# Both silu of a state-space block computed by ScalarE in one step, and a small projection spread over two phases into another PSUM bank

## The chip, the cores and the metric

The kernel runs on one core of a Trainium2 chip. The metric is the device time in microseconds (us), the median of three runs. The core has TensorE (PE), VectorE (DVE), ScalarE (ACT), GpSimd (POOL) and SyncE (SP), which issues the DMAs. Each works through its own list of instructions in order and waits on semaphores.

## The reference

All data is fp32. There are B = 4 batches of L = 512 tokens, model width E = 512, 16 states per channel.

```python
# block 1: selective scan, gated by z
z   = layernorm(x)                                  # per token
u   = silu(causal_conv4(in_proj(ctx)) + conv_b)     # 512 channels
dt, Bm, Cm = split(x_proj @ u)                      # 16 + 16 + 16 rows: the small projection
delta = softplus(dt_proj @ dt + dt_b)
state = state * exp(delta * A) + delta * u * Bm     # for each of 16 states, along 512 tokens
y   = sum_n(state * Cm) + D * u
x   = x + tanh(g_xattn) * (y * silu(z))
# block 2: a gated low-rank mixture of 32, top 2 of a softmax
h   = layernorm(x)
g   = top2(softmax(h @ Wr))
x   = x + tanh(g_ffn) * ((h @ U) * g) @ V * (0.9 + 0.2 * gate)
```

## The kernel before

The work of block 1 is cut into 20 phases f. Phases 0 to 11 take one batch b and one group k of 128 channels over all 512 tokens; the last batch is done in two halves of 256 tokens (phases 12 to 19). A phase has 16 positions n, one for each state. At each position ACT computes the decay (L1007, `exp`), DVE runs the scan (L1262), and the term added comes either from PE (`make_dbu`, L748, into one of three PSUM banks `p_s`) or from POOL (L558, a pair of states at once). POOL multiplies the scanned pair by C (L573; some pairs are done by DVE, L1280), and PE turns and sums it into `p_y` (L770). Which engine does which pair is a fixed table. Rings tie the engines together: three banks `p_s`, three buffers `da` for decays, twelve slots `state`, two buffers `dbu` on POOL.

Everything else is written by hand into a position of these phases: for the phase after it the dt projection (PE, n = 4), softplus (ACT, n = 6 to 8) and `delta` (DVE, L1221, n = 7); for the block five phases on the in-projection (PE, n = 9), the start of the convolution (ACT, L924, n = 12) and its three taps (DVE, L1204, n = 10 to 12); and block 2 of tile f - 5 or f - 6 (scores, top 2, products with U and V).

The two silu are made by halves, as v * (1 + tanh(v)) on halved inputs, since tanh lies in the same activation table as `exp`. For z, ACT writes `zh` (L1026) at n = 13 and `tanh` into the bank `p_v` (L1031) at n = 14, and DVE multiplies them at n = 14 (L1285). For u, ACT writes `tanh` into the bank `p_pr` (L933) and DVE multiplies (L1212), both at n = 15. The first four blocks of u are exceptions: they use the Silu function before the phases begin.

Phases 3, 7 and 11 are the last of their batch ("turning"). In them PE computes the small projection of the next batch (four products, L680, two at n = 1 and two at n = 2) into `p_pr`, ACT copies it to `xd` at n = 5 (L941), PE's dt projection waits for that copy at n = 4 (L692), and POOL writes diagonals of B (L531) and the scale of z (`scale_of_z`, L579 to L589, six small operations).

## Time and profile before

| | |
|---|---|
| median of 3 runs | 539.43 us (539.42 to 541.25) |
| the profiled execution | 541.24 us, its span 539.4 us |
| PE busy | 489.4 us, 91% of the span |
| DVE busy | 476.8 us, 88% |
| POOL busy | 454.4 us, 84% |
| ACT busy | 398.6 us, 74% |

The engines share the span almost evenly: no engine is idle for long between the first phase and the last, and a busy share says little without the stretch it comes from. The DMA queues move 73 GB/s on average and are quiet in most stretches. The busy time of PE counts its matmuls; weight loads run beside them.

### The profile page before, as it was taken

How to read it: one execution, taken by the hardware profiler on the slowest of the kernel's cores; microseconds unless marked ns; L12 is line 12 of the kernel's file. 1: busy time of each engine (PE TensorE's matmuls, PEld its weight loads, DVE VectorE, ACT ScalarE, POOL GpSimd, SP SyncE). 2: the span in 40 equal slices, each digit the busy share in tenths (PEclk: the TensorE clock that was granted, in tenths of full speed). 3: DMA queues.
4: the chain of work that ended last, by engine and by line, in shares of the span. 5: the costliest groups of instructions: out<-in, count | busy, mean ns of one | idle time of the engine just before them, and what ended most of it. 6: DMA issues, size and time to landing. Idle time of an engine off the chain costs nothing.

```text
span 539.4 us, 9244 instructions
## 1 busy us (share of the span) xinstructions
PE 489.4 (91%) x3018; PEld 367.8 (68%) x3018; DVE 476.8 (88%) x880; ACT 398.6 (74%) x726; POOL 454.4 (84%) x335
## 2 busy tenths in 40 slices
PE   9989798979677999999989999999899999899687
PEld 5569597758475776668677776667566666676654
DVE  3799999879899999789999999888988989999851
ACT  4698869386867777587968777577888898888542
POOL 1299999959999999979999999989799898987810
PEclk9979999999998999999998999999999999999799
DMA  5595001055220001074120000087000000000001
GB/s 134 161 373 215 0 2 40 2 200 192 82 78 2 1 0 60 7 280 169 59 80 2 19 2 21 5 299 227 22 21 1 21 20 21 2 20 21 1 19 39
DMA packets 18705, 39.36 MB, mean 73 GB/s; under 512 B 5586, under 2 KB 6354, under 8 KB 18659
## 3 DMA queue, kind: packets, MB, share of 16 engines
q1 hardware_dynamic: 18658, 38.79, 21.1%
q8 instruction: 24, 0.39, 0.3%
q14 instruction: 23, 0.18, 0.1%
HBM read 34.33 MB, written 4.46 MB: 72 GB/s over the span
## 4 chain that ended last, share of the span: by engine, by line
PE 54%; DVE 19%; ACT 18%; issue 8%; DVEq 0%; POOL 0%; ACTq 0%; POOLq 0%
PE p_s L748 12%; PE p_y L770 11%; DVE state L1262 9%; PE p_v L803 8%; PE p_f L794 6%; ACT da L1007 4%; PE p_tr L717 4%; PE p_pr L692 2%; PE p_pr L680 2%; DVE p_s L1262 2%; ACT p_s L1007 2%; DVE x L1204 2%; ACT pair_b L991 2%; PE p_pr L673 2%; PE p_f L783 2%
## 5 line engine op out<-in xcount | busy, mean ns | idle before, releaser
L573 POOL TENSOR_TENSOR state<-state,c_bc 128x1024 f32<-128x1024 f32 (+1 forms) x131 | 256.7, 1973 | 21.5 <-DVE state L1262 19.2
L748 PEld LDWEIGHTS p_s<-pair_b,du_t 128*128 128x128 f32 x1072 | 139.2, 198 | 44.7 <-issue 31.4
L748 PE MATMUL p_s<-pair_b,du_t 128*128 128x128 f32 x1072 | 153.1, 285 | 16.7 <-DVE state L1262 13.8
L770 PE MATMUL p_y<-ident,state 128*128 128x128 f32 x1024 | 149.5, 276 | 0.0
L558 POOL TENSOR_TENSOR dbu<-du,pair_b 128x1024 f32<-128x1024 f32 (+1 forms) x80 | 145.3, 1818 | 1.7 <-DVE p_s L1262 1.7
L1007 ACT ACTIVATE p_s<-delta,a_neg 128x512 f32<-128x512 f32 (+1 forms) x162 | 93.5, 580 | 65.8 <-DVE state L1280 33.0
L1262 DVE TENSOR_TENSOR_SCAN state<-da,p_s 128x512 f32<-128x512 f32 (+1 forms) x116 | 134.4, 1173 | 6.3 <-PE p_s L748 5.7
L770 PEld LDWEIGHTS p_y<-ident,state 128*128 128x128 f32 x1024 | 121.6, 144 | 23.7 <-issue 22.7
L1007 ACT ACTIVATE da<-delta,a_neg 128x512 f32<-128x512 f32 (+1 forms) x158 | 100.4, 648 | 14.0 <-DVE state L1262 13.7
L1262 DVE TENSOR_TENSOR_SCAN state<-p_s,dbu 128x512 f32<-128x512 f32 (+1 forms) x100 | 98.2, 997 | 1.8 <-POOL dbu L558 1.8
L794 PE MATMUL p_f<-u_sb,h_t 128*128 128x512 f32 x112 | 55.9, 602 | 0.5 <-DVE gw L1365 0.5
L803 PE MATMUL p_v<-v_sb,hug_t 128*128 128x512 f32 x112 | 55.3, 597 | 0.0
L1280 DVE TENSOR_TENSOR state<-p_s,c_bc 128x256 f32<-128x256 f32 (+1 forms) x58 | 30.6, 527 | 0.7
L531 POOL TENSOR_SCALAR_AFFINE_SELECT pair_b<-b_t 128x1024 f32<-128x1024 f32 x11 | 12.4, 1132 | 20.5 <-ACT b_t L964 20.5
L1262 DVE TENSOR_TENSOR_SCAN state<-p_s,carry,dbu 128x256 f32<-128x256 f32 x40 | 28.0, 735 | 0.5 <-POOL dbu L558 0.4
L1262 DVE TENSOR_TENSOR_SCAN p_s<-p_s,dbu 128x512 f32<-128x512 f32 x22 | 26.8, 1218 | 0.0
L794 PEld LDWEIGHTS p_f<-u_sb,h_t 128*128 128x128 f32 x112 | 18.8, 194 | 10.8 <-issue 9.8
L964 ACT ACTIVATE sz_t<-p_tr 128x512 f32<-128x512 f32 (+1 forms) x20 | 10.1, 507 | 21.4 <-PE p_tr L717 21.2
L1204 DVE SCALAR_TENSOR_TENSOR vsp<-p_pr,cw,vsp 128x511 f32<-128x511 f32 (+2 forms) x33 | 24.1, 731 | 1.1 <-ACT vsp L924 1.1
L759 PEld LDWEIGHTS p_y<-ident,skipped 128*128 128x128 f32 x64 | 7.3, 142 | 25.5 <-issue 25.5
L673 PE MATMUL p_pr<-cx,w_in 128*128 128x512 f32 x44 | 21.1, 601 | 3.4 <-DVE delta L1221 3.4
L1007 ACT ACT_TABLE_LOAD x18 | 23.1, 1283 | 0.3
(182 smaller groups left out, 687.8 us busy)
## 6 DMA issues: line engine op xcount, KB each, us to landing
c_bc<-bc_rows SPq DMA_DIRECT2D x32, 512.0 KB, 5.2
pair_b<-bc_rows SPq DMA_DIRECT2D x16, 512.0 KB, 5.7
xs<-in_x SPq DMA_DIRECT2D x16, 256.0 KB, 4.0
out<-ot SPq DMA_DIRECT2D x14, 256.0 KB, 2.0
cx<-in_ctx_t SPq DMA_DIRECT2D x4, 512.0 KB, 3.5
u_sb<-in_u_w SPq DMA_DIRECT2D x1, 1024.0 KB, 14.2
v_sb<-in_v_w SPq DMA_DIRECT2D x1, 1024.0 KB, 15.6
w_in<-in_in_w_t SPq DMA_DIRECT2D x1, 384.0 KB, 4.6
```

The lines of the kernel that those rows point to most:

```text
L558: eng.tensor_tensor(dbu[:, i % 2, :, 0:w], du[:, 0:w].unsqueeze(1).to_broadcast([P, 2, w]), rows_of_b(p)[:, :, c0:c0 + w], ALU.mult).then_ ...
L573: eng.tensor_tensor(pair, pair, c_bc[:, 2 * p:2 * p + 2, c0:c0 + w], ALU.mult).then_inc(po_cs, 1)
L673: mm = eng.matmul(conv_bank(q)[:, :], w_in[:, k, e * P:(e + 1) * P], cx[:, k, :], start=(k == 0), stop=(k == KD - 1))
L717: mm = eng.transpose(turn_bank(kind, i)[:, k, :], source[:, k * P:(k + 1) * P], ident[:, :])
L748: mm = eng.matmul(p_s[g % BANKS][:, t * P:(t + 1) * P], du_t[:, f % 2, t, :], diagonals_of(n // 2)[:, n % 2, c0 // P + t, :], start=(t == ...
L770: mm = eng.matmul(p_y[:, t, :], slot(NS * f + n)[:, t * P:(t + 1) * P], ident[:, :], is_transpose=True, start=False, stop=(n == NS - 1 and ...
L794: mm = eng.matmul(hu_bank(T)[:, :], ht_of(T)[:, k, :], u_sb[:, k, :], start=(k == 0), stop=(k == Q - 1))
L803: mm = eng.matmul(v_bank(T)[:, :], hugt_of(T)[:, k, :], v_sb[:, k, :], start=False, stop=(k == Q - 1), skip_group_check=True)
L1007: eng.activation(to, delta[:, f % 2, 0:w], ACT.Exp, scale=a_neg[:, k, n:n + 1]).then_inc(ac_da, 1)
L1204: eng.scalar_tensor_tensor(out=conv_v(q)[:, s:], in0=conv_bank(q)[:, 0:L - s], scalar=cw[:, q % Q, TAPS - 1 - s:TAPS - s], in1=conv_v(q)[: ...
L1262: eng.tensor_tensor_scan(scanned, decayed, added, first, ALU.mult, ALU.add).then_inc(ve_scan, 1)
L1280: eng.tensor_tensor(slot(g)[:, 0:w], scanned, c_bc[:, n, c0:c0 + w], ALU.mult).then_inc(ve_cs, 1)
```

## The change

Both silu are now one ScalarE instruction with the function Silu, which needs a table of its own. `silu(f)` loads the Silu table, does one or two blocks of z and up to two of u, and loads a table back that holds `exp` and `ln` together. It stands in 15 of the 20 phases: at n = 0 in phase 1 and in the turning phases, at n = 9 in the others, and only in every second phase of the last batch, with two blocks of z. DVE's two multiplications are gone, and ACT's `zh`, `tanh` of z and `tanh` of u with them. The convolution is now done in the slot of `u` itself, in a ring of 5 instead of 6. `tanh(g_xattn)` is no longer folded into the scale of z (`scale_of_z` has four operations instead of six) but applied where `sz_t` is copied.

The small projection of the next batch goes into `p_v`: three of its products stand at n = 13, 14 and 15 of the phase before the turning one, the fourth at n = 2 of the turning phase. `copy_small` moves from n = 5 to n = 4, the dt projection of a turning phase from n = 4 to n = 5, and `place_residual`, which starts the product with V in `p_v`, follows `copy_small`. Two small operations on `cw` and `cb` ahead of the phases are gone.

```diff
+    SILU_Z = {1: [0, 1]}
+    SILU_Z.update({f: [f] for f in range(2, SPLIT)})
+    SILU_Z.update({f: [f, f + 1] for f in range(SPLIT, F, 2)})
+    SILU_U = {1: [5], 2: [4, 6]}
+    SILU_U.update({f: [f + 4] for f in range(3, SPLIT)})
...
-            return x2[:, q // Q, q % Q, :] if q < 5 else vsp[:, :]
+            return x2[:, q // Q, q % Q, :] if q < 5 else u[:, q % U_RING, :]
...
             def scale_of_z(b):
...
-                eng.tensor_tensor(zv[:, 1, :], zv[:, 0, :], minus_half[:, :], ALU.pow).then_inc(po_zs, 1)
+                eng.tensor_tensor(zr[:, b % 2, 0, :], zv[:, 0, :], minus_half[:, :], ALU.pow).then_inc(po_zs, 1)
                 eng.wait_ge(po_zs, ZOPS * b + 2)
-                eng.tensor_tensor(zr[:, b % 2, 0, :], zv[:, 1, :], half[:, :], ALU.mult).then_inc(po_zs, 1)
-                eng.tensor_tensor(zv[:, 0, :], zv[:, 1, :], minus_half[:, :], ALU.mult).then_inc(po_zs, 1)
-                eng.wait_ge(po_zs, ZOPS * b + 4)
-                eng.tensor_tensor(zr[:, b % 2, 1, :], zmv[:, :, 0], zv[:, 0, :], ALU.mult).then_inc(po_zs, 1)
-                eng.wait_ge(po_zs, ZOPS * b + 5)
-                eng.wait_ge(ac_k, 2)
-                eng.tensor_scalar(zr[:, b % 2, 2:4, :], zr[:, b % 2, 0:2, :], gx[:, :], None, ALU.mult).then_inc(po_zs, 1)
+                eng.tensor_tensor(zv[:, 1, :], zmv[:, :, 0], zr[:, b % 2, 0, :], ALU.mult).then_inc(po_zs, 1)
+                eng.wait_ge(po_zs, ZOPS * b + 3)
+                eng.tensor_tensor(zr[:, b % 2, 1, :], zv[:, 1, :], minus_one[:, :], ALU.mult).then_inc(po_zs, 1)
...
@@ PE, small_projection and the phases
-                    wait_for_u(eng, Q * b + Q if b else k + 1)
-                    mm = eng.matmul(p_pr[0:BROW + 2 * NS, :], w_small[:, k, :], u[:, (Q * b + k) % U_RING, :],
+                    eng.wait_ge(ac_u, Q * b + k + 1)
+                    if b and k == 0 and Q * b - 8 >= 0:
+                        eng.wait_ge(ac_out, Q * b - 7)
+                    mm = eng.matmul(small_bank(b)[0:BROW + 2 * NS, :], w_small[:, k, :], u[:, (Q * b + k) % U_RING, :],
...
-                        if turning:
-                            small_projection(b + 1, range(0, 2))
...
-                            small_projection(b + 1, range(2, Q))
+                            small_projection(b + 1, [Q - 1])
...
-                    if n == 4 and f < LAST:
+                    if n == (5 if turning else 4) and f < LAST:
                         dt_projection(f + 1)
+                    if n >= 13 and k == Q - 2 and b + 1 < B:
+                        small_projection(b + 1, [n - 13])
...
@@ ACT
+            def silu_z(f):
...
+                eng.activation(zh_of(f), xs[:, b % 2, k, c0:c0 + w], ACT.Silu, bias=zr[:, b % 2, 1, k:k + 1],
+                               scale=zr[:, b % 2, 0, k:k + 1]).then_inc(ac_z, 1)
+            def silu(f):
+                eng.preload_act_table(ACT.Silu)
+                for i in SILU_Z[f]:
+                    silu_z(i)
+                for q in SILU_U.get(f, []):
+                    silu_u(q)
+                eng.preload_act_table_set("natural_log_exp_and_others")
...
+                    if n == 4 and turning:
+                        copy_small(b + 1)
+                        if tail >= 0:
+                            place_residual(tail)
...
-                    if n == 13:
-                        z_part(f, 0)
-                    if n == 14:
-                        z_part(f, 1)
...
-                        if f + 5 < BLOCKS:
-                            tanh_v(f + 5)
+                    if f in SILU_Z and n == (0 if f == 1 or turning else 9):
+                        silu(f)
...
@@ DVE
-                        silu_z(f)
...
-                    if f == 0 and n == 15:
-                        silu_u(4)
-                    if n == 15 and f + 5 < BLOCKS:
-                        silu_u(f + 5)
```

How the instructions then stand. First ACT in phase 6, from the second part of softplus for phase 7 to the start of the next convolution; `vsp` is softplus, `da` and `p_s` are decays, `skipped` is D * u. Before:

```order
201 L955 ACTIVATE vsp<-vsp 128x512
202 L1007 ACTIVATE da<-delta,a_neg 128x512
203 L958 ACT_TABLE_LOAD
204 L958 ACTIVATE vsp<-vsp 128x512
205 L1007 ACT_TABLE_LOAD
206 L1007 ACTIVATE da<-delta,a_neg 128x512
207 L1015 ACTIVATE skipped<-u,dsk 128x512
208 L1007 ACTIVATE p_s<-delta,a_neg 128x512
209 L1086 ACTIVATE ot<-p_v 128x512
```

The same place of the changed kernel:

```order
186 L963 ACTIVATE vsp<-vsp 128x512
187 L1016 ACTIVATE da<-delta,a_neg 128x512
188 L966 ACTIVATE vsp<-vsp 128x512
189 L1016 ACTIVATE da<-delta,a_neg 128x512
190 L1024 ACTIVATE skipped<-u,dsk 128x512
191 L1038 ACT_TABLE_LOAD
192 L1033 ACTIVATE zh<-xs,zr 128x512
193 L941 ACTIVATE u<-u 128x512
194 L1043 ACT_TABLE_LOAD
195 L1016 ACTIVATE p_s<-delta,a_neg 128x512
196 L1102 ACTIVATE ot<-p_v 128x512
```

The two table loads moved from around the last part of softplus to behind `skipped`, with the two silu between them, ahead of the decay of position 10.

Second, PE from the end of phase 6 into phase 7, a turning phase; `p_s<-pair_b,du_t` is `make_dbu`, `p_y<-ident,state` the sum of y, `p_tr` the transposes, `w_small` the small projection. Before:

```order
202 L717 MATMUL p_tr<-ident,du 128x128 x4
203 L770 MATMUL p_y<-ident,state 128x128 x8
204 L717 MATMUL p_tr<-ident,h 128x128 x4
205 L748 MATMUL p_s<-pair_b,du_t 128x128 x4
206 L770 MATMUL p_y<-ident,state 128x128 x4
207 L748 MATMUL p_s<-pair_b,du_t 128x128 x4
208 L770 MATMUL p_y<-ident,state 128x128 x4
209 L680 MATMUL p_pr<-u,w_small 64x512 x2
210 L770 MATMUL p_y<-ident,state 128x128 x4
211 L680 MATMUL p_pr<-u,w_small 64x512 x2
212 L717 MATMUL p_tr<-ident,zh 128x128 x4
213 L783 MATMUL p_f<-router,h_t 128x32 x4
```

The same place of the changed kernel:

```order
203 L691 MATMUL p_v<-u,w_small 64x512
204 L728 MATMUL p_tr<-ident,du 128x128 x4
205 L781 MATMUL p_y<-ident,state 128x128 x4
206 L691 MATMUL p_v<-u,w_small 64x512
207 L781 MATMUL p_y<-ident,state 128x128 x4
208 L691 MATMUL p_v<-u,w_small 64x512
209 L728 MATMUL p_tr<-ident,h 128x128 x4
210 L759 MATMUL p_s<-pair_b,du_t 128x128 x4
211 L781 MATMUL p_y<-ident,state 128x128 x4
212 L759 MATMUL p_s<-pair_b,du_t 128x128 x4
213 L781 MATMUL p_y<-ident,state 128x128 x8
214 L691 MATMUL p_v<-u,w_small 64x512
```

Three products of the small projection moved ahead of the first `make_dbu` of the turning phase; the fourth stays ahead of the scores.

## Rows read from the trace of the kernel before

**Rows 1.** The windows view, cut where DVE starts `delta` (L1221, position 7 of a phase).
```profile
core 0: us, PE busy (x) PEld busy (x) DVE busy (x) ACT busy (x) POOL busy (x), PEclk, DMA share, GB/s
63.26:87.24 23.98, 22.05 (x178) 19.69 (x177) 23.79 (x27) 19.05 (x29) 23.98 (x12) 1.00 0.01 2
87.24:117.25 30.01, 27.62 (x197) 21.79 (x195) 25.61 (x29) 20.32 (x31) 24.49 (x12) 1.00 0.19 66
...
173.96:202.58 28.62, 27.53 (x180) 21.42 (x179) 28.30 (x48) 21.35 (x35) 28.01 (x15) 1.00 0.00 1
202.58:234.15 31.57, 29.98 (x181) 20.99 (x181) 28.42 (x49) 22.87 (x38) 27.68 (x14) 1.00 0.20 74
...
324.06:355.18 31.12, 29.54 (x181) 20.97 (x180) 28.41 (x48) 22.40 (x39) 27.69 (x14) 1.00 0.15 49
...
380.69:488.94 108.25, 101.95 (x582) 70.55 (x581) 99.22 (x272) 93.45 (x199) 94.50 (x107) 1.00 0.04 16
```

**Rows 2.** The waits of POOL: releaser, us in total, times, longest.
```profile
POOL state L573 <- DVE state L1262: 19.2, 18, 5.5
POOL fr L596 <- DVE fmv L1317: 11.0, 3, 5.7
```

**Rows 3.** POOL's timeline: start, duration, and in brackets the idle time before.
```profile
113.33 2.36 POOL L573 TENSOR_TENSOR state<-state,c_bc 128x1024 f32<-128x1024 f32 x1 [5.52 <-DVE state L1262]
...
230.72 2.35 POOL L573 TENSOR_TENSOR state<-state,c_bc 128x1024 f32<-128x1024 f32 x1 [1.52 <-DVE state L1262]
...
```

**Rows 4.** POOL's timeline over the scale of z in phase 3.
```profile
128.61 0.20 POOL L583 TENSOR_TENSOR zr<-zv,half 128x4 f32<-128x4 f32 x1
...
129.34 0.31 POOL L589 TENSOR_SCALAR zr<-zr,gx 128x8 f32<-128x8 f32 x1
129.61 1.10 POOL L531 TENSOR_SCALAR_AFFINE_SELECT pair_b<-b_t 128x1024 f32<-128x1024 f32 x1
```

**Rows 5.** Groups by line on DVE, PE and ACT: count, busy us, mean ns, idle before.
```profile
L1285 DVE SCALAR_TENSOR_TENSOR zh<-p_v,zh 128x512 f32<-128x512 f32 (+1 forms) x20 | 11.2, 559 | 0.0
L1212 DVE SCALAR_TENSOR_TENSOR u<-p_pr,vsp 128x512 f32<-128x512 f32 x11 | 7.4, 670 | 0.0
L680 PE MATMUL p_pr<-u,w_small 128*64 128x512 f32 x32 | 15.9, 608 | 0.2 <-ACT u L929 0.2
L1007 ACT ACT_TABLE_LOAD x18 | 23.1, 1283 | 0.3
```

**Rows 6.** PE's timeline in phases 6 and 7, with the idle time before each piece.
```profile
215.41 0.65 PE L717 MATMUL p_tr<-ident,h 128*128 128x128 f32 x4 [1.09 <-ACT h L1046]
...
218.66 1.93 PE L680 MATMUL p_pr<-u,w_small 128*64 128x512 f32 x4
...
227.17 1.12 PE L692 MATMUL p_pr<-xd,w_dt 17*128 17x512 f32 x2 [0.49 <-ACT xd L941]
```

**Rows 7.** ACT's timeline in phase 6.
```profile
199.75 1.28 ACT L958 ACT_TABLE_LOAD   x1
201.04 0.63 ACT L958 ACTIVATE vsp<-vsp 128x512 f32<-128x512 f32 x1
...
204.22 0.67 ACT L1007 ACTIVATE p_s<-delta,a_neg 128x512 f32<-128x512 f32 x1
...
206.54 0.76 ACT L924 ACTIVATE vsp<-p_pr,cb,cw 128x512 f32<-128x512 f32 x1
...
207.81 0.81 ACT L1026 ACTIVATE zh<-xs,zr 128x512 f32<-128x512 f32 x1
```

**Rows 8.** DVE's timeline beside it: position 10 and the first tap.
```profile
206.58 1.21 DVE L1262 TENSOR_TENSOR_SCAN state<-p_s,dbu 128x512 f32<-128x512 f32 x1
...
208.29 0.73 DVE L1204 SCALAR_TENSOR_TENSOR vsp<-p_pr,cw,vsp 128x511 f32<-128x511 f32 x1
```

**Rows 9.** The same in phase 2: ACT's start of the convolution, DVE's first tap.
```profile
91.60 0.76 ACT L924 ACTIVATE vsp<-p_pr,cb,cw 128x512 f32<-128x512 f32 x1
92.39 0.75 DVE L1204 SCALAR_TENSOR_TENSOR vsp<-p_pr,cw,vsp 128x511 f32<-128x511 f32 x1
```

133 lines of the change are left out of this document (56 added, 77 removed).

## The prediction

> **What bounds the kernel now.** I read the busy shares first, and they decide nothing: four engines lie between 74% and 91%. So I cut the span into stretches of one phase and compared, in each, its length with every engine's busy time [rows 1]; the reader is to look for the engine whose busy time comes nearest to the length. In phases 1 to 2 (the first stretch) it is POOL, 23.98 of 23.98 us, with DVE at 23.79. In phases 5 to 6 all three are within a hair: DVE 28.30, POOL 28.01 and PE 27.53 of 28.62. In the stretches that enter a turning phase the picture differs: 30.01, 31.57 and 31.12 us long, POOL works only 24.49, 27.68 and 27.69 of them, while PE works 27.62, 29.98 and 29.54. In the last batch (seven half phases, 108.25 us) PE has 101.95, DVE 99.22, POOL 94.50. So no engine is the bound alone: POOL and DVE share it in ordinary phases, PE has it in turning ones and in the last batch.
>
> Next I read the waits of POOL, because POOL is never ahead for long: between the first phase and the last it waits 19.2 us for scans, and 11.0 us for the statistics of block 2, of which 5.7 lie behind the last phase [rows 2]. That is 24.5 us, and the change can gain little more than that, since it takes almost no work from POOL. Its largest single waits are in the turning phases: 5.52 us in phase 3, and in phase 7 the longest of several is 1.52 [rows 3].
>
> **The change part by part.**
>
> *DVE loses the two multiplications.* 20 of z, 11.2 us, and 12 of u (11 in the row, one more of the same size), 8.1 us [rows 5]: 19.3 us of busy time. A full phase loses 2 x 0.67, and since neighbours on DVE overlap by some 0.08 each, 1.17 us; a half phase about 0.3. In phases 5 to 6 that puts DVE at 27.1 of 28.62, but POOL's 28.01 stays: the phase can shorten by 0.6, not by 1.17. In phases 1 to 2 it can shorten by nothing. Over the six ordinary full phases 4 to 6 and 8 to 10 the bounds are 0 and 6 x 1.17 = 7.0; I take **-2.0**, nearer to POOL's row than to DVE's.
>
> *POOL loses two of six operations of the scale of z.* From L583 to the diagonal behind L589 are 129.61 - 128.61 = 1.00 us for four operations [rows 4]; two small ones, the second waiting for the first, take some 0.55. That is 0.45 in each of three turning phases, on the engine that has no idle time just behind them: **-1.35**. The fourth scale stands ahead of the phases beside other work and counts nothing.
>
> *The small projection.* Two of its products take 1.93 us on PE, less 0.07 of overlap [rows 6], so all four take 3.7 (the mean of one part is 608 ns before overlap, two parts to a product [rows 5]), and 2.8 of that moves to n = 13 to 15 of the phase before. This removes no PE work, and PE has no lead to hide it in: it feeds a ring of three banks. The stretch that enters phase 7 holds both the old and the new place and PE's 29.98 us fill it to 1.59. What the move can give is that idle time: PE waited 1.09 us for `h` just ahead of phase 7's first `make_dbu`, and 0.49 for `xd` ahead of the dt projection [rows 6]. With two products ahead of the transpose of `h`, and `tanh` of u gone from ACT ahead of `h`, the first wait is covered; with `xd` copied one position earlier and the dt projection one later, so is the second. I count 1.6 for phase 7 and the same for phase 11 (31.12 - 29.54). In phase 3 the stretch leaves PE 2.4 us, but part of what ended POOL's wait of 5.52 there is the scans of positions 3 to 5, and ACT will be late (below), so I count 0.7, with bounds of 0 and 2.4. Together **-3.9**. If the first wait were not covered, each of the later two would give 0.5 less than 1.
>
> *ACT.* Before, 37 table loads in the phases (18 ahead of `exp` [rows 5], as many ahead of `ln`, one in phase 0), now 30; each holds ACT 1.29 us (199.75 to 201.04) [rows 7]. The two loads stay in an ordinary full phase, but move from around the last part of softplus to behind `skipped`, and bring silu of z (like L1026, 0.70 after overlap) and of u (like L958, 0.53). So the decay of position 10 comes 1.3 us later than now relative to position 6. In phase 6 it is ready at 204.89 and its scan begins at 206.58, a cover of 1.7 [rows 7, 8]: enough. The convolution's start ends at 207.30, the tap that needs it begins at 208.29, a cover of 1.0: DVE is late by 0.3. In phase 2 two blocks of u are in the group, 1.85 us more, and the cover is 0.03 (92.36 to 92.39) [rows 9]: DVE loses about 1.9 there, against 1.17 gained. In the turning phases the group of 3.9 us stands behind the decay of position 0; what is queued behind it is the decay of position 1, for which DVE waits, and behind that the copies of `h` and `sz`. PE comes late at the same place by its 2.8 us, so the two lie side by side. In the last batch half of the loads go and ACT gains. POOL's full queue in phases 1 to 2 absorbs part of phase 2's loss. Bounds 0 and 1.9 + 6 x 0.3 = 3.7, I take **+1.0**.
>
> The Trainium skill states another price for the loads: in "ScalarE: Activation LUTs", What ACT_TABLE_LOAD costs, about 1283 ns and then about 1380 ns of drain for each switch. The trace agrees with the first (1.28) and shows no second: the instruction behind the load begins at its end. By that rule a group would hold ACT 2.8 us longer than I count.
>
> *The last batch.* PE idles 108.25 - 101.95 = 6.3 us in it; part of that is waiting for scans or for ACT's copies. DVE loses 0.3 and ACT about 1.8 us a half phase (one load of 1.28, and two writes of `zh` and `tanh` made one). Bounds 0 and 6.3, I take a third: **-2.1**.
>
> *At nothing:* the ring of u at 5 (its last reader stands three positions ahead of the write, on the same engine, and POOL's read is a phase old), the scale in the copy of `sz_t` (another [128,1] operand, some 0.1 us on ACT, eight positions ahead of its use), `place_residual` behind `copy_small`, and the two small DVE operations ahead of the phases, where ACT decides.
>
> **Sum:** -2.0 - 1.35 - 3.9 + 1.0 - 2.1 = -8.35 us. The profiled execution took 541.24, 1.8 above the median of the runs; it would come to 532.9, and the median to **531**.
>
> **The rivals.**
>
> *DVE's whole cut arrives.* For it: in phases 5 to 6 DVE is busier than POOL. Against it: POOL's 23.98 of 23.98 in phases 1 to 2. It gives about 11 x 1.17 + 8 x 0.3 = 15 us, the scale 1.35, and the waits of PE at the turns 3: 520.
>
> *Almost nothing arrives.* PE's work is the same to the last matmul, and it fills 94 to 95% of the turning stretches and of the last batch. If its remaining 1.6 and 6.3 us are the price of handing over between engines and not waits that go away, only -1.35 and half of the ordinary phases' 2.0 remain, and ACT's +1.0 against them: 538.
>
> *ACT's group becomes the new stall (slower).* Place: n = 10 of the ordinary full phases and n = 1 of the turning ones. For it: the covers of 0.03 and 1.0. Against it: in phase 6 the group costs only 0.3 beyond its cover. Price: if each of the eleven groups of phases 1 to 11 made DVE wait as in phase 2, 1.9 each, the loss is 21, the DVE cut there 11 x 1.17 = 12.9, the turns and the scale 5.3: +3, 542.5 or more. It decides from the point where a group delays the tap by more than the cover of 1.0 and DVE's 1.17 together, that is when it holds ACT 2.2 us longer than the loads do now, not 1.3. The drain of the page cited above would do just that.
>
> **How the numbers follow.** The sum as described 0.68 (its own range 527 to 535.5), the whole DVE cut 0.06, almost nothing 0.17, slower 0.09. 0.5% is 2.7 us, about what a measurement of this kernel can tell from no change: faster means under 536.7, slower over 542.1. A few hundredths of the third case fall below 536.7 and of the fourth below 542.1: faster 0.76, same 0.16, slower 0.08. The range leaves out the second case, half of the fourth and some of both edges: 526 to 539.
>
> **What the profile after would show.** DVE busy down by 17 to 19 us; 30 table loads in the phases, each followed at once by its activation. The stretches entering phases 7 and 11 at 30 us or a little under, with no wait of PE for `h` or `xd`; the one entering phase 3 shorter by 1 to 2. Phases 1 to 2 not shorter, with DVE waiting 1 to 2 us for ACT's convolution in phase 2. Ordinary full phases 0 to 0.6 us shorter with POOL as good as never idle. The last batch at 106. Wrong would be: POOL idle in ordinary phases (then ACT or PE, not POOL, took over from DVE), DVE waiting for decays at n = 10 or 11 in most phases, or a turning stretch that stays at 31.

## The result and the profile after

The changed kernel takes **534.03 us** (median of 4 runs, 533.25 to 534.77), the kernel before beside it 539.59 (4 runs): ratio 0.9881, 95% interval 0.9856 to 0.9906. That is 5.6 us less by the medians, 6.4 by the ratio, and 0.9 to 1.4% by the interval. The forecast was 531, with a range of 526 to 539. The profiled execution took 533.53, 7.7 less than that of before; the sum had said 8.35 less.

The page of the kernel after, its busy times:

```profile
span 531.8 us, 9178 instructions
PE 491.4 (92%) x3018; PEld 368.0 (69%) x3018; DVE 462.9 (87%) x846; ACT 380.1 (71%) x699; POOL 451.9 (85%) x327
```

DVE's busy time fell by 13.9 us (476.8 to 462.9), ACT's by 18.5, PE's and POOL's hardly. The windows view of the kernel after, cut as in [rows 1] where DVE starts `delta`, now L1226. The first two stretches run from there in the start to position 7 of phase 0 and of phase 1; the last is what lies behind the last cut.

```profile
core 0: us, PE busy (x) PEld busy (x) DVE busy (x) ACT busy (x) POOL busy (x), PEclk, DMA share, GB/s
23.17:39.16 15.99, 13.68 (x66) 11.31 (x65) 15.22 (x18) 13.83 (x33) 13.69 (x11) 0.68 1.01 356
39.16:66.06 26.90, 24.62 (x172) 21.99 (x171) 22.35 (x25) 21.82 (x38) 25.68 (x12) 0.88 0.32 118
90.03:119.06 29.03, 27.57 (x194) 21.26 (x193) 24.57 (x27) 22.77 (x34) 22.30 (x12) 1.00 0.16 50
174.64:203.36 28.72, 27.66 (x180) 21.19 (x179) 27.07 (x46) 22.08 (x35) 28.45 (x16) 1.00 0.00 1
203.36:234.04 30.68, 30.68 (x183) 20.98 (x182) 27.22 (x46) 23.30 (x37) 29.22 (x15) 1.00 0.24 84
320.12:351.49 31.37, 31.37 (x189) 21.85 (x188) 27.33 (x47) 24.15 (x39) 28.15 (x15) 1.00 0.21 66
375.20:482.93 107.73, 101.74 (x582) 70.62 (x581) 97.73 (x268) 84.17 (x187) 95.02 (x107) 1.00 0.04 16
482.93:531.80 48.87, 39.96 (x204) 27.39 (x202) 29.88 (x79) 22.77 (x50) 20.94 (x20) 0.97 0.06 22
```

Two stretches of the kernel before that [rows 1] doesn't hold, in the same view: the first two.

```profile
23.78:38.26 14.48, 11.80 (x68) 10.29 (x67) 13.83 (x17) 13.61 (x32) 14.15 (x12) 0.76 1.02 345
38.26:63.26 25.00, 23.22 (x182) 20.32 (x181) 23.87 (x29) 21.00 (x38) 24.38 (x12) 1.00 0.40 151
```

Two stretches got longer by more than 0.3 us, and the forecast had looked at neither: the one of phase 0 by 1.5 us and the one of phases 0 to 1 by 1.9. In the turning stretches of phases 7 and 11 PE fills the stretch to the last hundredth (30.68 of 30.68, 31.37 of 31.37). The table cuts the whole profiled span of five kernels in this way; three are experiments below ("DVE cut alone" is the kernel before without the two multiplications, so that silu is left out and tanh alone stands in its place, "DVE work back" the kernel after with DVE's load of before, "both repairs" the kernel after mended at two places). A turning stretch stands together with the one behind it, for the runs showed that a gain in one is often taken back in the other.

| stretch (phases) | before | DVE cut alone | after | DVE work back | both repairs |
|---|---|---|---|---|---|
| start, to `delta` of phase 0 | 23.78 | 23.14 | 23.17 | 23.81 | 23.20 |
| 0 | 14.48 | 15.59 | 15.99 | 15.99 | 14.96 |
| 0 to 1 | 25.00 | 23.20 | 26.90 | 26.34 | 23.23 |
| 1 to 2 | 23.98 | 23.98 | 23.97 | 23.80 | 23.58 |
| 2 to 4 (turn at 3) | 57.22 | 56.07 | 56.09 | 56.12 | 56.09 |
| 4 to 6 | 58.12 | 57.88 | 57.24 | 61.01 | 57.25 |
| 6 to 8 (turn at 7) | 62.02 | 61.54 | 59.41 | 60.61 | 59.95 |
| 8 to 10 | 59.46 | 57.53 | 57.35 | 59.70 | 57.34 |
| 10 to 12 (turn at 11) | 56.63 | 56.46 | 55.08 | 54.66 | 55.23 |
| last batch | 108.25 | 107.95 | 107.73 | 108.85 | 107.61 |
| behind it | 50.46 | 49.36 | 48.87 | 49.21 | 49.26 |
| span | 539.4 | 532.7 | 531.8 | 540.1 | 527.7 |

POOL's waits after, against [rows 2]:

```profile
POOL state L586 <- DVE state L1267: 19.2, 19, 4.8
POOL fr L605 <- DVE fmv L1316: 9.2, 3, 4.4
```

POOL waits as long for scans as before. So the time did not come out of these waits, on which the argument for a small gain had rested. What POOL has less is 2.5 us of busy time, 1.8 of waits for the statistics of block 2, and 1.7 us of waits for DVE ahead of its own products, which are gone.

**Where phase 1 lost.** ACT's and DVE's timelines of the kernel after, in phase 1:

```profile
50.39 1.28 ACT L1038 ACT_TABLE_LOAD   x1
51.69 1.52 ACT L1033 ACTIVATE zh<-xs,zr 128x512 f32<-128x512 f32 x2
53.12 0.61 ACT L941 ACTIVATE u<-u 128x512 f32<-128x512 f32 x1
53.75 1.28 ACT L1043 ACT_TABLE_LOAD   x1
55.04 1.95 ACT L1016 ACTIVATE da<-delta,a_neg 128x512 f32<-128x512 f32 x3
...
55.85 1.22 DVE L1267 TENSOR_TENSOR_SCAN state<-da,p_s 128x512 f32<-128x512 f32 x1 [2.12 <-PE p_s L759]
```

The view names PE's `p_s` as releaser, but the scan starts 0.16 us behind the end of the first of ACT's three decays at 55.04, and that decay stands behind the group of 4.6 us (two loads, silu of z twice, silu of u). DVE waits 2.12 us at this place. The timeline also shows what a load costs: 1.28 us, and the activation starts at its end.

PE waits in its turn, 2.17 us for the scan, and then works at a clock that differs from one kernel to the next. Its first `make_dbu` behind this wait, in the kernel after and in the one with POOL's wait (below):

```profile
60.28 2.05 PE L759 MATMUL p_s<-pair_b,du_t 128*128 128x128 f32 x8 [2.17 <-DVE state L1267]
...
59.85 1.13 PE L760 MATMUL p_s<-pair_b,du_t 128*128 128x128 f32 x8 [2.17 <-DVE state L1268]
```

In the first the granted clock is 0.50 from 60 to 66 us, the lower level of 1.2 GHz, and DVE waits another 1.34 and 0.28 us for `p_s`; in the second it stays at 1.00 and DVE waits no more. The stretch of phases 0 to 1 takes 26.90 us in the first and 25.34 in the second, with the same group at the same place. So of the 3.7 us that the kernel after loses here against DVE's cut alone (23.20), about 2.1 are the wait behind the group and about 1.6 the lower clock behind it.

### The profile page after: what moved, and what is told of

The parts are those of the page before. It is cut to its first block, busy times and chain, and to the rows that moved or that the text cites. A ratio compares the mean times of both kernels' runs of the same rounds, so it can differ in the third digit from the quotient of the medians.

```text
span 531.8 us, 9178 instructions
## 1 busy us (share of the span) xinstructions
PE 491.4 (92%) x3018; PEld 368.0 (69%) x3018; DVE 462.9 (87%) x846; ACT 380.1 (71%) x699; POOL 451.9 (85%) x327
## 4 chain that ended last, share of the span: by engine, by line
PE 48%; POOL 19%; DVE 13%; ACT 10%; issue 9%; DMA 1%; DVEq 0%; SPq 0%; POOLq 0%; ACTq 0%
PE p_s L759 12%; PE p_y L781 11%; POOL state L586 9%; POOL dbu L571 7%; DVE state L1267 6%; PE p_v L814 5%; PE p_f L805 5%; PE p_tr L728 3%; PE p_v L691 2%; ACT da L1016 2%; DVE x L1216 2%; PE p_pr L703 2%; ACT pair_b L1000 1%; PE p_f L794 1%; PE p_pr L682 1%
## 5 line engine op out<-in xcount | busy, mean ns | idle before, releaser
L759 PEld LDWEIGHTS p_s<-pair_b,du_t 128*128 128x128 f32 x1072 | 140.7, 200 | 44.9 <-issue 33.4
L1016 ACT ACTIVATE da<-delta,a_neg 128x512 f32<-128x512 f32 (+1 forms) x158 | 99.3, 647 | 18.5 <-DVE state L1267 18.4
L805 PEld LDWEIGHTS p_f<-u_sb,h_t 128*128 128x128 f32 x112 | 18.5, 191 | 12.7 <-issue 9.6
L1216 DVE SCALAR_TENSOR_TENSOR u<-p_pr,cw,u 128x511 f32<-128x511 f32 (+2 forms) x33 | 24.1, 730 | 2.2 <-ACT u L936 2.1
L814 PEld LDWEIGHTS p_v<-v_sb,hug_t 128*128 128x128 f32 x112 | 18.1, 190 | 8.4 <-issue 8.3
L556 POOL TENSOR_TENSOR du<-delta,u 128x512 f32<-128x512 f32 (+1 forms) x19 | 19.8, 1043 | 2.8 <-POOL dbu L571 2.8
```

The costliest lines, as they stand in the source:

```text
L556: eng.tensor_tensor(du[:, 0:w], delta[:, f % 2, 0:w], u[:, (Q * b + k) % U_RING, c0:c0 + w], ALU.mult).then_inc(po_du, 1)
L759: mm = eng.matmul(p_s[g % BANKS][:, t * P:(t + 1) * P], du_t[:, f % 2, t, :], diagonals_of(n // 2)[:, n % 2, c0 // P + t, :], start=(t == ...
L805: mm = eng.matmul(hu_bank(T)[:, :], ht_of(T)[:, k, :], u_sb[:, k, :], start=(k == 0), stop=(k == Q - 1))
L814: mm = eng.matmul(v_bank(T)[:, :], hugt_of(T)[:, k, :], v_sb[:, k, :], start=False, stop=(k == Q - 1), skip_group_check=True)
L1016: eng.activation(to, delta[:, f % 2, 0:w], ACT.Exp, scale=a_neg[:, k, n:n + 1]).then_inc(ac_da, 1)
L1216: eng.scalar_tensor_tensor(out=conv_v(q)[:, s:], in0=conv_bank(q)[:, 0:L - s], scalar=cw[:, q % Q, TAPS - 1 - s:TAPS - s], in1=conv_v(q)[: ...
```

## The experiments

All ratios are against the kernel before on the same chip (541.5 to 542.2 us there). The kernel after ran again beside three of them (534.27 us, ratio 0.9863: the split group, POOL's wait, and DVE's work with one input in PSUM). It did not run beside "both repairs", "scale of z back" and "DVE's cut alone"; these are compared with 534.27 us and 0.9863 across chips, and medians and ratios then differ by about 1 us.

### Small projection back in the turning phase

```
@@ PE, n loop
+                    if n == 1 and turning:
+                        small_projection(b + 1, range(0, 2))
...
-                            small_projection(b + 1, [Q - 1])
+                            small_projection(b + 1, range(2, Q))
...
-                    if n >= 13 and k == Q - 2 and b + 1 < B:
-                        small_projection(b + 1, [n - 13])
```

> The changed kernel with the small projection back in the turning phases alone, two products at n = 1 and two at n = 2, still in p_v. Theory (the move pays only through PE's waits for h and for xd, some 1.1 and 0.5 us a turn before, since PE's work is the same): +1 to +2 us against the changed kernel, 535 to 536, and PE waits again for h or xd at the turns. Rival (the move is what the change lives on): +4 us or more, 538 or above. Rival (it does nothing, the silu alone do it): within 0.5 us.

Measured 534.56 us, ratio 0.9861 (0.9831 to 0.9891): the same as the kernel after, so the second rival (within 0.5 us) has it. PE does wait again for `h`, 0.57 us in phase 7 and 0.57 in phase 11, as the theory said. In its profile phases 6 to 8 take 60.28 us instead of 59.41, phases 2 to 4 56.19 instead of 56.09, 10 to 12 55.22 instead of 55.08: 1.1 us in all. But 0.9 of it lies in phases 6 to 8, where kernels with the small projection in its new place take anything from 59.41 to 60.09 us. So the profile shows 0.2 us for the spreading of the small products outside that scatter, and the median 0.3 to 0.5.

### DVE's work back, both inputs in SBUF

```
+            def multiply_again(f, w):
+                eng.scalar_tensor_tensor(out=vsp[:, 0:w], in0=delta[:, f % 2, 0:w], scalar=1.0,
+                                         in1=delta[:, f % 2, 0:w], op0=ALU.add, op1=ALU.mult).then_inc(ve_again, 1)
...
+                        multiply_again(f, PHASE[f][3])
...
+                    if n == 15 and f + 5 < BLOCKS:
+                        multiply_again(f, L)
```

> The changed kernel, and DVE does again as much work as before: a multiplication of the same size into a spare buffer at n = 14 of each phase and at n = 15 where u was multiplied (33 in all, 19 us; their result is not used). Theory (DVE was the limit only in part of the ordinary phases, POOL and PE take over): +3 to +5 us, 537 to 539, not 19. Rival (DVE's cut gives nothing, the gain is of the turns and of ACT): below +1. Rival (DVE decides everywhere): +10 or more.

Measured 566.15 us, ratio 1.0450 (1.0397 to 1.0503). By the number that is the last rival's "+10 or more", but three times it, and more than the 19 us of work that was meant to be put back: 32 operations cost 32 us, a full microsecond each. The groups of DVE in its profile show why this was no measure of DVE's cut:

```profile
L1295 DVE SCALAR_TENSOR_TENSOR vsp<-delta 128x512 f32<-128x512 f32 x24 | 35.8, 1493 | 0.2 <-issue 0.2
```

The operation that the change removed took 670 ns at this size [rows 5]; it read one input from PSUM. This one reads both from SBUF and takes 1493 ns in the mean, up to 2830, and POOL's busy time rises with it, from 452.3 us in the experiment before to 463.5, with no work added to POOL. I repeated it with one input in PSUM (further below).

### No table loads in the phases

```
-                eng.activation(u[:, q % U_RING, :], conv_v(q), ACT.Silu).then_inc(ac_u, 1)
+                eng.activation(u[:, q % U_RING, :], conv_v(q), ACT.Silu if q < Q else ACT.Identity).then_inc(ac_u, 1)
...
-                eng.preload_act_table(ACT.Silu)
...
-                eng.preload_act_table_set("natural_log_exp_and_others")
```

> The changed kernel without the 30 table loads of the phases: in them Identity stands in the place of Silu, so silu is left out of the result, and ACT's group at n = 0 or 9 is 2.6 us shorter. Theory (the group makes DVE wait at n = 1 of phase 1 and of the turning phases and at n = 10 of phases 2 and 8, 2.1, 2.0, 1.3, 1.0, 1.0 and 0.7 us in the trace): -4 to -6 us against the changed kernel, 528 to 530. Rival (POOL's queue and PE's work cover these waits): within 1 us.

Measured 531.15 us, ratio 0.9797 (0.9766 to 0.9827). This kernel leaves out silu. It takes 3.4 us less than the first experiment, which ran beside it and equals the kernel after: all 30 loads (38.5 us of ACT) together cost 3.4 us, less than the theory's 4 to 6 and more than the rival's 1. The windows view says where:

```profile
39.64:62.75 23.11, 22.27 (x176) 19.89 (x177) 22.03 (x25) 18.92 (x36) 22.88 (x11) 1.00 0.38 139
199.79:230.49 30.70, 30.70 (x182) 21.00 (x181) 27.45 (x46) 19.59 (x34) 29.12 (x15) 1.00 0.23 82
371.55:479.37 107.82, 101.80 (x582) 70.61 (x581) 97.77 (x267) 76.21 (x182) 94.67 (x107) 1.00 0.04 16
```

Phases 0 to 1 fall from 26.90 to 23.11 us. Phases 6 to 7 stay at 30.70 and the last batch at 107.82, although ACT works 3.7 and 8.0 us less in them. Nearly all that the loads cost is at this one place (3.0 us against the first experiment, whose stretch took 26.15); of the other places where the theory saw DVE wait, phases 8 to 10 come next with 0.5.

### The loads doubled

```
                 eng.preload_act_table(ACT.Silu)
+                eng.preload_act_table_set("natural_log_exp_and_others")
+                eng.preload_act_table(ACT.Silu)
```

> The changed kernel with four table loads in each of the 15 groups instead of two: ACT held 2.6 us longer at each place. Theory (the covers at n = 10 and n = 1 are used up: 0.1 to 0.8 us in the full phases, 0.7 to 1.2 in the last batch): +12 to +25 us, slower than the kernel before. Rival (ACT has 28% of the span idle and the groups are covered elsewhere by POOL and PE): below +6.

Measured 568.49 us, ratio 1.0487 (1.0443 to 1.0531): 34 us for 30 more loads of 1.28, 38.5 us of ACT, beyond the theory's 12 to 25. The groups of ACT, one of the two added lines:

```profile
L1039 ACT ACT_TABLE_LOAD x15 | 19.2, 1283 | 0.1
```

Together with the experiment before, this measures the covers. The first 30 loads cost 3.4 us; the next 30 find the covers used up and cost nearly their own length. The turning stretches, which hold two groups each and so 5.1 us of added loads, grow from 29.03 to 35.00 and from 30.68 to 35.39 us, the ordinary ones of phases 4 to 5 and 5 to 6, with one group, by 3.1 and 1.4. The granted clock in these four is 0.95, 0.90, 0.93 and 0.91, so part of the 34 us is PE at its lower clock; how much was not separated.

### The kernel after once more

> The changed kernel once more, beside the three that follow, so that they are compared on one chip. Every theory: 534 us, give or take 1, and in the profile the same stretches as before: 26.9 us for phase 0 to 1's stretch with DVE idle 4.5 us, 16.0 us for the stretch ahead of it.

Measured 534.27 us (6 runs, 533.44 to 535.12), ratio 0.9863 (0.9839 to 0.9886). Its stretches are those of the table within 0.1 us but for four: the start at 23.64, phases 0 to 1 at 26.39, 1 to 2 at 23.59, and 49.88 behind the last batch. So the two ends of the span differ by 0.5 and 1.0 us between two profiles of one kernel.

### Phase 1's group split and moved

```
-    SILU_Z = {1: [0, 1]}
+    SILU_Z = {0: [0], 1: [1]}
...
-                    if f in SILU_Z and n == (0 if f == 1 or turning else 9):
+                    if f in SILU_Z and n == (0 if turning else 9 if f else 13):
```

> Silu of z of phase 0 goes into a group of its own at n = 13 of phase 0, and phase 1 has its group (z of phase 1, u of block 5) at n = 9 as the other ordinary phases; no group stands at n = 0 of phase 1. One group more, so two table loads more. Theory that the place of phase 1's group costs about 3 us (the scan of n = 1 waited 2.1 us for the decay queued behind it): 531.0 to 532.5, the stretch that holds phase 1 at 23.5 to 24.5 us instead of 26.9, at most 0.7 us given back in phase 0 and at n = 10 of phase 1. Rival, that the ACT work costs the same wherever it stands (the loads in ACT's queue, not their place): 534 to 536.

Measured 532.77 us, ratio 0.9832 (0.9806 to 0.9857): 1.5 us less than the kernel after, just outside the theory's range of 531.0 to 532.5. The stretch of phases 0 to 1 falls by 3.2 us as the theory said, and part of it is given back at two places:

```profile
39.12:62.34 23.22, 21.65 (x173) 19.52 (x174) 22.14 (x25) 20.38 (x36) 22.99 (x11) 1.00 0.36 135
62.34:86.58 24.24, 22.60 (x181) 20.03 (x180) 22.55 (x25) 18.54 (x28) 24.24 (x12) 1.00 0.01 2
171.22:201.18 29.96, 29.39 (x179) 22.52 (x178) 27.33 (x47) 20.58 (x33) 29.69 (x16) 0.92 0.00 1
```

Phases 1 to 2 take 24.24 us instead of 23.59 and DVE idles 1.7 of them: the group at n = 9 of phase 1 is longer than the cover behind it. Phases 5 to 6 take 29.96 instead of 28.72 with the granted clock at 0.92 instead of 1.00, and phases 6 to 7 take 31.36 instead of 30.67.

### POOL's diagonals behind DVE's first products

```
             scale_of_z(0)
+            eng.wait_ge(ve_dbu, 2)
             diagonals(0, 2)
```

> POOL makes its second and third diagonal tile only after DVE's two first products of du and B (one wait of POOL on DVE added; no work changed). In the changed kernel POOL's two fewer operations of the z scale let these diagonals start 1.7 us earlier, beside DVE's two products, which took 1184 and 1570 ns instead of 687. Theory that the two engines take turns at SBUF there, and that this cost the stretch of phase 0 its 1.5 us: the two products at 0.69 each again, the stretch at 14.5 to 15.0 instead of 16.0, 532.5 to 533.5 in all. Rival, that POOL's later start costs as much as DVE gains: 534, same within 0.5.

Measured 533.10 us, ratio 0.9842 (0.9815 to 0.9870). First the timelines of DVE and POOL of the kernel after at this place, and of the kernel before:

```profile
25.32 2.68 DVE L1272 TENSOR_TENSOR dbu<-du,pair_b 128x512 f32<-128x512 f32 x2 [0.73 <-DMA pair_b<-bc_rows]
24.87 2.58 POOL L544 TENSOR_SCALAR_AFFINE_SELECT pair_b<-b_t 128x1024 f32<-128x1024 f32 x2
...
25.81 1.30 DVE L1267 TENSOR_TENSOR dbu<-du,pair_b 128x512 f32<-128x512 f32 x2 [0.61 <-DMA pair_b<-bc_rows]
26.57 2.55 POOL L531 TENSOR_SCALAR_AFFINE_SELECT pair_b<-b_t 128x1024 f32<-128x1024 f32 x2
```

Before, POOL's six operations of the scale of z held its diagonals until 26.57, when DVE's two products were nearly done. After, with four operations, POOL starts them at 24.87, 0.45 ahead of DVE, and DVE's products, with both inputs in SBUF, take 2.68 us instead of 1.30. With the wait they take 1.29 again (DVE, timeline of this experiment), and POOL's two diagonals 2.14:

```profile
26.28 1.29 DVE L1273 TENSOR_TENSOR dbu<-du,pair_b 128x512 f32<-128x512 f32 x2 [1.00 <-DMA pair_b<-bc_rows]
27.65 2.14 POOL L544 TENSOR_SCALAR_AFFINE_SELECT pair_b<-b_t 128x1024 f32<-128x1024 f32 x2 [2.02 <-DVE dbu L1273]
```

The stretch of phase 0 falls from 15.98 to 14.86 us, and the next from 26.39 to 25.34, where PE kept its higher clock (above). The median moved by 1.2 only: in the profiled execution phases 6 to 7 take 31.35 us instead of 30.67, and phases 5 to 6 take 30.10 us instead of 28.72, again with a clock of 0.92. The windows view there, first of this kernel, then of the kernel after once more, 1.9 us later in its span:

```profile
170.00:172.00 2.00, 0.65 (x1) 0.50 (x2) 1.93 (x5) 1.98 (x3) 2.00 (x2) 0.65 0.00 0
172.00:174.00 2.00, 2.00 (x3) 0.66 (x2) 2.00 (x3) 1.97 (x4) 2.00 (x2) 0.50 0.01 4
...
172.00:174.00 2.00, 0.78 (x2) 0.49 (x3) 1.93 (x5) 1.98 (x3) 2.00 (x2) 1.00 0.00 0
174.00:176.00 2.00, 2.00 (x12) 1.34 (x11) 2.00 (x4) 1.97 (x4) 2.00 (x2) 1.00 0.01 4
```

In the one TensorE is granted 0.50, its level of 1.2 GHz, and in the other 1.00, 2.4 GHz. PE had idled 1.71 and 1.47 us just ahead in the one, 1.72 and 1.43 in the other. In the first full 2 us the one has 3 matmuls and the other 12 in the stretch that answers to it.

### DVE's work back, one input in PSUM

```
+            def multiply_again(w):
+                eng.scalar_tensor_tensor(out=vsp[:, 0:w], in0=p_pr[:, 0:w], scalar=1.0,
+                                         in1=vsp[:, 0:w], op0=ALU.add, op1=ALU.mult).then_inc(ve_again, 1)
...
+                    if n == 14 and f < LAST:
+                        multiply_again(PHASE[f + 1][3])
+                    if n == 15 and f + 5 < BLOCKS:
+                        multiply_again(L)
```

> DVE's whole cut put back: 19 multiplications at n = 14 and 11 at n = 15 of the same form as those removed (one input in PSUM, one in SBUF, out to SBUF), on data that nothing else needs; ACT, PE and POOL have the work of the changed kernel. If DVE's cut gave what I forecast for the ordinary phases, and a little elsewhere: 536 to 538, that is 2 to 4 us more. If DVE is the real bound of the ordinary phases: 30 x 0.6 = 17 us more, 545 to 551. If the cut was worth nothing because POOL and PE decide: 534, same within 0.5. DVE busy up by about 17 us in each case.

Measured 542.04 us (12 runs), ratio 1.0021 (1.0001 to 1.0042): **all of the gain is gone**. The time lies between the expectations, above the 536 to 538 of my forecast and below the 545 of DVE as the bound. The group of the added operation on DVE, and the windows of phases 4 to 5 and 6 to 7:

```profile
L1247 DVE SCALAR_TENSOR_TENSOR vsp<-p_pr,vsp 128x512 f32<-128x512 f32 (+1 forms) x30 | 17.8, 594 | 0.0
...
146.06:176.40 30.34, 22.89 (x153) 17.96 (x152) 29.45 (x53) 20.66 (x32) 29.98 (x18) 0.91 0.12 36
207.07:237.75 30.68, 30.68 (x183) 20.98 (x182) 28.51 (x49) 24.77 (x39) 27.69 (x14) 1.00 0.24 85
```

17.8 us of DVE's time cost 7.8 us of the kernel's. In the table, the cost lies in phases 4 to 6 (3.8, of which by my estimate about 1.4 belong to the stretch of phases 5 to 6, with a clock of 0.93 and 30.67 us; that is what the lower clock cost there in the kernel with POOL's wait), 8 to 10 (2.4), 7 to 8 (1.2) and the last batch (1.1). Phases 0 to 1 and 2 to 4 take as long as without it, within 0.1 us. Where phase 7 is entered it costs nothing: 30.68 us with the work and 30.68 without, for PE fills both.

### Both repairs together

The two edits above, with phase 1's group at n = 12 instead of 9:

```
+                    if f in SILU_Z and n == (0 if turning else 9 if f > 1 else 13 - f):
```

> Both repairs together: silu of z of phase 0 in a group at n = 13 of phase 0, phase 1's group at n = 12 (behind the start of the convolution, not ahead of it), and POOL's wait for DVE's first two products. Theory that the two losses are apart from each other: 14.9 us for the stretch of phase 0 (16.0 in the changed kernel) and 23.2 for the next (26.4), with no wait of DVE at n = 10 of phase 1, so 529.5 to 531; up to 2 us of it can go again if TensorE's clock falls to its lower level in phase 5, as it did with either repair alone. Rival, that whatever is gained early is given back at the next turning phase: 532.5 to 534.

Measured **529.21 us** (528.45 to 529.55), ratio 0.9785 (0.9759 to 0.9812). This beats both kernels, 2.15% under the kernel before and 4 to 5 us under the kernel after (4.2 by the ratios, 5.1 by the medians). The windows of its stretches of phase 0 and of phases 1 to 2; the one between them takes 23.23 us:

```profile
23.20:38.16 14.96, 11.57 (x71) 9.68 (x69) 13.82 (x17) 13.82 (x33) 12.60 (x10) 0.89 1.02 353
61.39:84.97 23.58, 22.09 (x178) 19.72 (x178) 23.02 (x25) 18.71 (x28) 23.58 (x11) 1.00 0.01 2
```

POOL works 23.58 of 23.58 us in phases 1 to 2. Phases 5 to 6 stay at 28.73 here, with a clock of 0.96 in them and not 0.92.

### POOL's two operations of the scale of z back

```
                 eng.tensor_tensor(zr[:, b % 2, 1, :], zv[:, 1, :], minus_one[:, :], ALU.mult).then_inc(po_zs, 1)
+                if b:
...
+                    eng.tensor_tensor(z_again[:, 0, :], zr[:, b % 2, 0, :], minus_half[:, :], ALU.mult).then_inc(po_again, 1)
+                    eng.wait_ge(po_again, 2 * b - 1)
...
+                    eng.tensor_scalar(z_again[:, :, :], zr[:, b % 2, :, :], gx[:, :], None, ALU.mult).then_inc(po_again, 1)
```

> The changed kernel with POOL's two fewer operations of the z scale put back for batches 1 to 3, on data that nothing needs (one small product and the product with gx, waits as before the change). My term of -1.35 (0.45 in each of three turning phases): 535.5 to 536, and the stretches from phase 3 to 4, 7 to 8 and 11 to 12 each about 0.45 us (up to 1.0) longer. Rival, that POOL has room there because PE's 30.7 us set the turning phases: 534, same within 0.5.

Measured 535.35 us (534.86 to 535.62), ratio 0.9903 (0.9876 to 0.9929): 1.1 us more than the kernel after by the medians, 2.2 by the ratios, across chips. Phases 3 to 4 grow from 27.05 to 27.63 us and 11 to 12 from 23.74 to 24.30, 7 to 8 not at all (28.75 to 28.77). In the first two POOL hardly idles:

```profile
118.61:146.24 27.63, 22.37 (x170) 19.09 (x169) 24.32 (x27) 19.29 (x35) 27.30 (x21) 1.00 0.57 200
352.30:376.60 24.30, 22.44 (x148) 17.25 (x148) 20.57 (x43) 16.98 (x39) 23.48 (x22) 1.00 0.65 217
```

### The kernel before with DVE's cut alone

```
-                eng.activation(conv_bank(q)[:, :], conv_v(q), ACT.Tanh).then_inc(ac_th, 1)
+                eng.activation(u[:, q % U_RING, :], conv_v(q), ACT.Tanh).then_inc(ac_th, 1)
...
-                        silu_z(f)
...
-                        silu_u(f + 5)
```

> The kernel before with DVE's part of the change alone: its two multiplications are gone and tanh is used in their place, so silu is left out from block 4 of u on and in every gate; all of ACT's loads, the small projection and the z scale stay where they were. Theory that DVE's cut alone is the gain and that the rest of the change nets to nothing: 533 to 535.5, the stretches of phases 4 to 6 and 8 to 10 shorter by 0.6 to 1.2 each, turning stretches by 0.5 at most. Rival, that POOL holds the ordinary phases as I forecast (2.0 us in six): 539 to 540.

Measured 534.72 us, ratio 0.9894 (0.9866 to 0.9922). This kernel leaves out silu: `tanh` alone stands for it in every gate and from block 4 of u on. DVE's cut alone gives 6.9 us by the medians and 5.7 by the ratio, where the whole change gave 7.2 and 7.4 beside the kernel before on another chip. The total is the theory's, the places are only half of them: phases 8 to 10 give 1.9 us, but 4 to 6 only 0.2. Its windows of phases 0 to 1, 3 to 4 and 5 to 6:

```profile
38.73:61.93 23.20, 21.84 (x175) 19.69 (x176) 22.11 (x26) 21.04 (x38) 22.97 (x11) 1.00 0.39 143
115.91:141.98 26.07, 21.26 (x163) 18.39 (x162) 24.31 (x26) 20.74 (x37) 25.74 (x20) 1.00 0.59 205
170.58:199.86 29.28, 28.19 (x179) 21.57 (x178) 27.32 (x46) 21.11 (x35) 29.01 (x16) 0.96 0.00 1
```

### The dt projection back at n = 4

```
-                    if n == (5 if turning else 4) and f < LAST:
+                    if n == 4 and f < LAST:
...
-                    if n == 4 and turning:
-                        copy_small(b + 1)
...
                     if n == 5:
...
+                        if turning:
+                            copy_small(b + 1)
```

> The changed kernel with the dt projection of the turning phases back at n = 4 on PE and the copy of the small projection back at n = 5 on ACT, behind the copy of the gated rows; the residual goes behind it, since it uses the same bank. The turning stretches got 1.0 to 2.6 us shorter by the change, and neither the place of the small products nor the loads nor DVE's cut gave it in the stretch of phases 2 to 3 (29.1, 29.0 there without each of them, 30.0 with DVE's cut alone). Theory that this one position is what took PE's wait for xd away: 535.5 to 537, the stretches entering phases 3, 7 and 11 each 0.5 to 1.0 us longer, and PE waiting about 0.5 us for xd again. Rival, that the wait only shows elsewhere: 534.3, same within 0.5.

Measured 534.39 us, ratio 0.9861 (0.9839 to 0.9883): the same as the kernel after. PE's timeline in phase 3 shows the wait back, as the theory said:

```profile
113.87 1.12 PE L703 MATMUL p_pr<-xd,w_dt 17*128 17x512 f32 x2 [0.89 <-ACT xd L949]
```

The stretch of phases 2 to 3 grows from 29.03 to 29.79 us. But the next falls from 27.06 to 26.30, and phases 2 to 4 take 56.09 with it and without it. The wait was real and removing it gave nothing; the rival was right.

## Why the prediction was right and where it was wrong

The direction and the range were right, and the total missed by 3 us. In the profiled executions, for which the sum was made, it came within 0.6 us (532.9 forecast, 533.53 measured); the other 2.3 us come from taking over that the profiled execution lies 1.8 above the median, as it did before. After, it lies 0.5 below. That the sum came so near is in good part luck, for terms that missed by 0.9 to 1.6 us cancel. They are, in the profiled executions:

| term of the sum | forecast | measured | what the runs say of it |
|---|---|---|---|
| ordinary full phases 4 to 6, 8 to 10 | -2.0 | -0.9 - 2.1 = -3.0 | DVE's cut, mis-sized |
| scale of z | -1.35 | -1.1 (in the row below too) | put back: +1.1 in the median |
| small projection and turns | -3.9 | -5.3 with the scale | sum right, parts wrong |
| ACT's lateness | +1.0 | +1.9 in phases 0 to 1 | wrong place |
| last batch | -2.1 | -0.5 | mis-sized |
| not in the sum: start and phase 0 | 0 | -0.6 + 1.5 | DVE beside POOL |
| not in the sum: behind the last batch | 0 | -1.6 | -0.6 in the second profile |

Without the row of the scale the measured column adds up to the -7.6 us of the spans.

**DVE's cut** was the step that failed most, by its places more than by its size there. The forecast said that an ordinary phase "can shorten by 0.6, not by 1.17" because POOL's 28.01 of 28.62 us stays, gave the six ordinary phases 2.0 us, and left the other full phases at nothing. Two experiments from opposite sides, removing it from before (-6.9 by the medians, -5.7 by the ratio) and adding it to after (+7.8), say that it is worth some 6 to 8 us, most of the whole change. It is not the whole cut either: 15 us would have been the first rival's. The two do not agree on the places. Taken away from before, it gives 1.9 us in phases 8 to 10, 1.1 in 3 to 4, and 1.8 in 0 to 1 against 1.1 lost in phase 0; 1.7 of the 6.7 us of the spans lie at the two ends, which scatter by as much. Put back into the kernel after, it costs 3.8 in phases 4 to 6 and 2.4 in 8 to 10, and 0.2 in 0 to 4. Only phases 8 to 10 are the same in both, so how a microsecond of DVE is priced in one given phase stays open.

What the runs show is why POOL's share was no floor. With DVE's cut alone POOL's busy time in phases 0 to 1 falls from 24.38 to 22.97 us and in 3 to 4 from 26.88 to 25.74, and in 2 to 3 it rises from 24.49 to 25.68, while over the whole span it is 454.1 us as against 454.4. A stretch is cut where DVE starts `delta`; when DVE comes earlier, the cut moves along POOL's queue, and part of POOL's work falls on the other side. POOL also gets its input from DVE, and DVE worked 23.87 us of the 25.00 in phases 0 to 1. That two engines that feed each other and are each near full set the time together is my reading of this; no run here tests it by itself. The four ordinary phases moved by -1.0, +0.1, -0.1 and -2.0 us: the one from which the forecast's 0.6 was read got no shorter.

**The turning stretches.** The pairs of stretches gave 1.13 + 2.61 + 1.55 = 5.3 us, and 1.35 + 3.9 = 5.25 had been forecast. But the reasons were mostly others. DVE's cut alone gives 1.15, 0.48 and 0.17 of it, the scale of z 1.1, the spreading of the small products 0.2 to 1.1, and the swap of the dt projection nothing, though it did remove PE's wait of 0.5 to 0.9 us for `xd` ([rows 6], and as predicted no such wait stands in phase 7 after). The forecast added up waits of PE; in phases 2 to 4 what was gained at the turn is taken back in the stretch behind it. About 0.7 us of the pairs 6 to 8 is no property of a kernel's edit: the stretch of phases 6 to 7 is 30.68 us in the kernel after, in the experiments without loads and with DVE's work back, and 31.36 in four others, with ordinary phases ahead of it that are alike. I didn't find what decides this. It may be part of the 1.3 to 2.2 us that the four sums leave of the 5.3; the rest of that was not isolated.

**ACT.** The forecast put 1.9 us into phase 2 and did not count phase 1. Phase 2's group stands at n = 9, in the stretch of phases 2 to 3, and DVE did wait behind it, for the decay of position 10 and for the start of the convolution:

```profile
95.42 1.22 DVE L1267 TENSOR_TENSOR_SCAN state<-p_s,dbu 128x512 f32<-128x512 f32 x1 [1.31 <-issue]
97.30 0.75 DVE L1216 SCALAR_TENSOR_TENSOR u<-p_pr,cw,u 128x511 f32<-128x511 f32 x1 [0.65 <-ACT u L936]
```

These 1.96 us are the 1.9 of the forecast, and they cost nothing: without any loads DVE waits only 0.72 us there, for POOL, and the stretch takes 29.04 us, with the loads 29.03. Phase 1 lost 1.9 us against before and 3.7 against the kernel with DVE's cut alone (26.90 and 23.20), of which the clock made about 1.6. The step that failed is "PE comes late at the same place by its 2.8 us, so the two lie side by side", since it was taken for every group at n = 0. In phases 3, 7 and 11 the wait is there too (DVE idles 1.31, 2.24 and 2.60 us at position 1, and the scan starts only 0.1 to 0.2 us behind the end of its decay), but the stretches that enter phases 3 and 7 stay as long without any loads (29.04 and 30.70 us); the one that enters phase 11 is 0.7 shorter then (30.70), with 0.6 of it taken back in the next. Phase 1 has the same place without a turn, and PE has nothing extra to do there. With the group split and moved this is gone. The main argument against the slower rival held: the groups in phases 2 to 11 cost next to nothing, and each load is followed at once by its activation, 30 of them with 1283 ns each. At n = 9 of phase 1, where the split put one, DVE waits 1.00 and 0.65 us behind it and the stretch is 0.65 us longer. The Trainium skill's "ScalarE: Activation LUTs", What ACT_TABLE_LOAD costs, adds some 1380 ns of drain to each; the trace disagrees, and so does the time of the doubled loads (34 us for 38.5 us of loads).

**POOL's scale of z** gave its 1.35 nearly (1.1). At the place that the forecast put at nothing, ahead of the phases, POOL came 1.7 us earlier with its diagonals and met DVE's two products. Of these 1.7 us, 0.6 are an earlier start of everything (POOL's first diagonal at 21.98 instead of 22.59) and 0.6 the two operations; the other 0.5 is the last of the six, which took 0.82 us before, beside DVE's first product, and 0.31 in the kernel with DVE's cut alone. That kernel still has all six operations and shows 2.19 us for DVE's products too, and a stretch of 15.59 us against 14.48: the margin had been 0.5 us before. So the experiment with POOL's wait shows what the overlap costs, 1.1 us, but not that the two operations brought it about; a shift of half a microsecond does.

**The last batch** has 6.3 us of idle PE before and 6.0 after. It is neither ACT's (8.0 us less work of ACT left it at 107.82) nor mainly DVE's (1.1 us with DVE's whole load back). The third of PE's idle time that the forecast took was not based on a wait that the change removes. PE waits there for scans (2.3 us) and for `x` (2.4), in short waits of up to 1.0 each; before it was 2.0 and 2.4, so they stay.

**The prediction's signs.** Right: the 30 loads, the turning stretches without PE's waits for `h` and `xd`, phase 3's stretch shorter by 1.0, phases 1 to 2 not shorter, POOL as good as never idle in ordinary phases, DVE waiting 1 to 2 us behind the group of phase 2 (1.96, with 0.65 of it for the convolution). Wrong: the last batch at 106, the ordinary phases each 0 to 0.6 us shorter, the stretch entering phase 11 at 30 (31.37, where the forecast had named a turning stretch that stays at 31 as a sign against it), and DVE's busy time, which fell by 13.9 and not 17 to 19. The 19.3 less 0.08 of overlap for each of 32 operations, and 1.4 more in the two products of phase 0, make 15.3 of it. The overlap was nearer to 0.11: the 17.8 us put back with one input in PSUM raised DVE's busy time by 14.5, over 30 operations. With that it is 14.4.

## What to carry to other kernels

Where several engines that hand work to each other are all near full, take the busy share of the second one for no floor, and price a cut on either by putting it back or taking it out, not by the gap between the two shares: here 17.8 us of DVE's work added cost 7.8 us and 19.3 us removed gave 6 to 7, something like 0.4 of it. Ask for each place of a rescheduled group what is queued behind it and how long its cover is, the odd first phase included, and add no wait at a turn to the sum before looking at what the next stretch then waits for. When a wait of one engine makes TensorE idle, look at the granted clock behind it: the wait can cost twice. When an engine gets ahead, look at what it now runs beside: a shift of half a microsecond between POOL and DVE cost 1.1 us at one place until a wait put the two in order.

## What the runs showed of the chip

**DVE beside POOL.** A 128x512 operation of DVE with both inputs in SBUF took 684 and 693 ns alone (with POOL's wait), 1184 and 1570 beside POOL's `affine_select`, and 1493 in the mean of 24 put among POOL's work. POOL is slowed as well: its two `affine_select` took 2.58 us beside them and 2.14 alone. The same form with one input in PSUM took 594 ns in the mean of 30, eight of them half as wide, and 670 at this size. The Trainium skill names this in "GPSIMD Engine Reference", Specifications: POOL shares its SBUF interfaces with VectorE, with contention for DVE instructions that have two SBUF inputs. The traces agree. A stand-in for a removed operation has to have its kinds of operands: 32 of the wrong kind cost 32 us, 30 of the right one 7.8.

**The clock.** Behind the same wait of PE, 2.17 us in phase 1, TensorE was granted 0.50 from 60 to 66 us in the kernel after and 1.00 in the kernel with POOL's wait, and the stretch took 26.90 us in the one and 25.34 in the other. The kernel after once more lies between, with 0.50 from 62 to 64 and 26.39 us. It went the other way in phase 5. In the profile of the kernel with POOL's wait TensorE was granted 0.50 from 171.3 to 177 us, and in that of the kernel after 1.00 over the same instructions, with PE's idle times just ahead the same within 0.04 us. The stretch took 1.4 us more. A repair that moves the work by a microsecond can meet this or miss it: either repair alone met it in its profiled execution (0.92 in phases 5 to 6) and gained 1.2 to 1.5 us in the median; with both together it was 0.96 there, the stretch stayed at 28.73 us, and the median gained 4 to 5. That the clock explains the medians too is argued from one profile of each, not shown.
